# A block of gate and up in one pass, and the last LoRA unit woven with two down units

## What is computed

```python
h = layernorm(x) * (1 + ca) + sa
x = x + ga * scan_block(h)                 # selective scan, 16 states per feature
h = layernorm(x) * (1 + cb) + sb
gate = h @ gate_w.T + (h @ gate_a.T) @ gate_b.T
up   = h @ up_w.T   + (h @ up_a.T) @ up_b.T
hidden = silu(gate) * up                   # 2752 wide
x = x + gb * (hidden @ down_w.T + (hidden @ down_a.T) @ down_b.T)
```

## Time and profile before

| | |
|---|---|
| median of three runs | 2287.67 us |
| the profiled execution | 2279.5 us |
| its span | 2277.7 us |
| mean granted TensorE clock | 0.947 |
| busy: PE, PEld | 2044.7 us (90%), 1860.5 us (82%) |
| busy: DVE, ACT, POOL | 1442.4 (63%), 1041.2 (46%), 1542.8 (68%) |
| matmuls | 11652 |
| the chain that ended last, by engine | PE 55%, DVE 13%, POOL 9%, ACT 8%, issue 7%, DMA 6% |

### The profile page before, as it was taken

One profiled execution on the slowest core, in us unless ns is written; L12 is line 12 of the kernel. 1 busy time (PEld: TensorE's weight loads), 2 busy tenths in 40 slices (PEclk: granted clock), 3 DMA queues, 4 the chain that ended last, 5 costly groups with the idle time before them and its releaser, 6 DMA issues.

```text
span 2277.7 us, 33011 instructions
## 1 busy us (share of the span) xinstructions
PE 2044.7 (90%) x11652; PEld 1860.5 (82%) x11652; DVE 1442.4 (63%) x2119; ACT 1041.2 (46%) x2330; POOL 1542.8 (68%) x960
## 2 busy tenths in 40 slices
PE   7587756878879989899999899999899999999999
PEld 4233235778869989799999799999799999999999
DVE  4665776778767878767778667778667774211111
ACT  3776765666554555444545344555343332210000
POOL 1578779998988877877867777867869895110100
PEclk9688877989989999999999999999999999999999
DMA  9799875778967768586768586768587877787786
GB/s 361 301 359 342 309 289 211 279 266 277 340 248 277 255 241 283 207 274 219 246 225 280 178 280 224 242 224 284 171 268 257 280 258 256 253 287 275 253 291 218
DMA packets 121204, 602.99 MB, mean 265 GB/s; under 512 B 10576, under 2 KB 23120, under 8 KB 80464
## 3 DMA queue, kind: packets, MB, share of 16 engines
q1 hardware_dynamic: 121040, 600.89, 75.0%
HBM read 514.63 MB, written 86.21 MB: 264 GB/s over the span
## 4 chain that ended last, share of the span: by engine, by line
PE 55%; DVE 13%; POOL 9%; ACT 8%; issue 7%; DMA 6%; DVEq 0%; SPq 0%; ACTq 0%; POOLq 0%
PE FP L780 48%; DVE ring L1186 5%; POOL ring L1300 4%; PE FP L663 4%; POOL y L1275 2%; DVE ring L1071 2%; DMA raw<-w_gu 2%; ACT SC L851 2%; DVE FP L1161 2%; DMA wts<-w_scratch 2%; PE FP L804 1%; POOL wts L1283 1%; ACT sqb L969 1%; PE FP L741 1%; DMA w_scratch<-wts 1%
## 5 line engine op out<-in xcount | busy, mean ns | idle before, releaser
L780 PE MATMUL FP<-xhi,wts 128*128 128x368 f32 (+2 forms) x4320 | 1078.4, 326 | 62.9 <-ACT dtb L974 29.6
L780 PEld LDWEIGHTS FP<-xhi,wts 128*128 128x128 f32 x4320 | 774.1, 194 | 73.2 <-issue 61.5
L1300 POOL TENSOR_TENSOR ring<-ring,c_row 128x736 f32<-128x736 f32 (+2 forms) x336 | 575.7, 1714 | 236.0 <-ACT hst L868 235.7
L780 PE MATMUL FP<-xlo,wts 128*128 128x368 f32 (+2 forms) x2160 | 700.3, 324 | 0.0
L851 ACT ACTIVATE SC<-dtb,aneg 128x368 f32<-128x368 f32 (+2 forms) x768 | 409.4, 538 | 592.9 <-DVE ring L1186 592.6
L780 PE MATMUL FP<-hhi,wts 128*128 128x368 f32 (+5 forms) x2376 | 571.1, 321 | 27.6 <-POOL hlo L1315 23.2
L1186 DVE TENSOR_TENSOR_SCAN ring<-SC,hst,ring 128x368 f32<-128x368 f32 (+1 forms) x640 | 579.3, 946 | 3.6 <-ACT SC L851 3.6
L1275 POOL TENSOR_TENSOR y<-y,ring 128x736 f32<-128x736 f32 (+1 forms) x320 | 554.7, 1733 | 13.9
L780 PEld LDWEIGHTS FP<-hhi,wts 128*128 128x128 f32 (+1 forms) x2376 | 406.7, 185 | 34.9 <-POOL hlo L1315 22.3
L780 PEld LDWEIGHTS FP<-xlo,wts 128*128 128x128 f32 x2160 | 418.8, 194 | 1.1
L780 PE MATMUL FP<-hlo,wts 128*128 128x368 f32 (+5 forms) x1188 | 379.4, 319 | 0.0
(11 more groups left out here) (104 smaller groups left out, 1929.7 us busy)
## 6 DMA issues: line engine op xcount, KB each, us to landing
wts<-w_scratch SPq DMA_DIRECT2D x249, 1152.0 KB, 5.3
wts<-w_scratch SPq DMA_DIRECT2D x91, 896.0 KB, 5.0
wts<-w_scratch SPq DMA_DIRECT2D x51, 1024.0 KB, 5.5
w_scratch<-wts SPq DMA_DIRECT2D x44, 1152.0 KB, 8.6
raw<-w_gu SPq DMA_DIRECT2D x44, 576.0 KB, 6.8
modw<-mod_w SPq DMA_DIRECT2D x24, 1024.0 KB, 10.4
w_scratch<-wts SPq DMA_DIRECT2D x16, 896.0 KB, 6.8
w_scratch<-wts SPq DMA_DIRECT2D x9, 1024.0 KB, 7.8
```

Of the source, the lines that this page charges most:

```text
L780: last = mm(out, w, x, start=(start and k == 0 and e == 0), stop=(stop and k == n - 1 and e == 2))
L1300: G.tensor_tensor(buf, buf, over_pair(c_of(k)), ALU.mult).then_inc(g_hc, 1)
```

## The change

Three things change.

1. Gate and up of block 21 are one unit `both`: 64 columns of gate and 64 of up weights side by side, 25 matmuls instead of 50. There are 71 units. The up half comes out on partitions 64 to 127 of the bank; ScalarE copies it to `tda[0:64]` (new line 1041), and VectorE multiplies from there (new line 1241).
2. The third `lora_down` and the first two `down` units of that part are woven on TensorE: all but the last block of `lora_down`, all but the last block of down 0, the last block of `lora_down`, all but the last of down 1, then the last blocks of down 0 and down 1.
3. The pieces of those two `down` units move ahead of that `lora_down`, on all engines.

```diff
-        UNITS += [("gate", part, j), ("up", part, j)]
+        UNITS += [("gate", part, j), ("up", part, j)] if j < NH - 1 else [("both", part, j)]
...
+    for u in (LAST_LORA + 1, LAST_LORA + 2):
+        at[LAST_LORA] += at[u]
+        at[u] = []
     return at
...
-            g = item[1] * NU + item[2] + (2 if UNITS[item[2]][0] == "gate" else 1)
+            g = item[1] * NU + item[2] + (2 if UNITS[item[2]][0] == "gate" or item[2] == LAST_LORA else 1)
...
-                    unit(c, u)
+                    if u == LAST_LORA:
+                        for v, step in ((u, "begin"), (u + 1, "begin"), (u, "end"), (u + 2, "begin"), (u + 1, "end"), (u + 2, "end")):
+                            unit(c, v, step)
+                    elif u not in (LAST_LORA + 1, LAST_LORA + 2):
+                        unit(c, u)
...
+                elif kind == "both":
+                    act.wait_ge(pe_unit, g + 1)
+                    act.wait_ge(g_hlo, c * NH + j - 1)
+                    A(hid[0:HALF, j % 2, 0:T], FP[0:HALF, BANK["unit", c, u], 0:T], ACT.Tanh, scale=0.5).then_inc(a_th, 1)
+                    A(tda[0:HALF, 0:T], FP[HALF:P, BANK["unit", c, u], 0:T], ACT.Copy).then_inc(a_up, 1)
...
+                elif kind == "both":
+                    h = hid[0:HALF, j % 2, 0:T]
+                    dve.wait_ge(a_th, c * NH + j + 1)
+                    V.scalar_tensor_tensor(out=h, in0=h, scalar=1.0, in1=FP[0:HALF, BANK["unit", c, u], 0:T], op0=ALU.add, op1=ALU.mult).then_inc(v_half, 1)
+                    dve.wait_ge(v_half, c + 1)
+                    dve.wait_ge(a_up, c + 1)
+                    V.scalar_tensor_tensor(out=h, in0=h, scalar=0.5, in1=tda[0:HALF, 0:T], op0=ALU.mult, op1=ALU.mult).then_inc(v_used, 1)
...
+    w_gu[NH - 1, 0, :, :, HALF:] = w_gu[NH - 1, 1, :, :, 0:HALF]
```

More of the change, by code:

```diff
@@ L57 @@
     for j in range(k0 + (part > 0), min(k1 + 1, NH)):
-        UNITS += [("gate", part, j), ("up", part, j)]
+        UNITS += [("gate", part, j), ("up", part, j)] if j < NH - 1 else [("both", part, j)]
     UNITS += [("lora_down", part, 0)] + [("down", part, m) for m in range(ND)]
 NU = len(UNITS)
-LAST_UP = max(u for u, unit in enumerate(UNITS) if unit[0] == "up")
+BOTH = max(u for u, unit in enumerate(UNITS) if unit[0] == "both")
+HALF = HID % P
+assert 2 * HALF == P
 GU_COLS = (ND + 1) * P
@@ L81, in lo_cols @@
     n = PARTS[part][1] - PARTS[part][0]
-    return {"lora_a": ND * P, "gate": GU_COLS, "up": GU_COLS, "lora_down": n * TD_COLS, "down": n * P}[kind]
+    return {"lora_a": ND * P, "gate": GU_COLS, "up": GU_COLS, "both": GU_COLS, "lora_down": n * TD_COLS, "down": n * P}[kind]
 def raw_cols(u):
@@ L91, in passes @@
     n = PARTS[part][1] - PARTS[part][0]
-    return {"lora_a": 3 * ND, "gate": 3 * ND + 1, "up": 3 * ND + 1}.get(kind, 3 * n)
+    return {"lora_a": 3 * ND, "gate": 3 * ND + 1, "up": 3 * ND + 1, "both": 3 * ND + 1}.get(kind, 3 * n)
 LN_ORDER = [(0, 0), (0, 1), (1, 0)] + [x for c in range(1, CHUNKS) for x in ([(0, c + 1)] if c + 1 < CHUNKS else []) + [(1, c)]]
@@ L270 @@
 SCAN_SHARE = 0.985
+LAST_LORA = unit_at("lora_down", len(PARTS) - 1, 0)
 def pieces_at(c):
@@ L781, in products, with unit @@
                 return last
-            def unit(c, u):
+            def unit(c, u, step=None):
                 kind, part, j = UNITS[u]
@@ L788, in unit @@
                 k0, k1 = PARTS[part]
[L789 to L794, removed]
+                if step != "end":
+                    if g in OTF:
+                        pe.wait_ge(a_hi, OTF.index(g) + 1)
+                        pe.wait_ge(g_lo, OTF.index(g) + 1)
+                    else:
+                        pe.wait_ge(d_w[s], 16 * loads_until(g))
+                    bank_free(pe, "unit", c, u)
                 if kind == "lora_a":
                     pe.wait_ge(g_h2, PAIRS * (c + 1))
-                if kind in ("lora_a", "gate", "up"):
+                if kind in ("lora_a", "gate", "up", "both"):
                     out = FP[:, bank, 0:T]
@@ L811, in unit @@
                     out = FP[0:w, bank, 0:T]
-                    products(out, pairs[:-1], stop=False)
+                    if step != "end":
+                        if kind == "lora_down":
+                            pe.wait_ge(g_hlo, c * NH + k1 - 1)
+                        products(out, pairs[:-1], stop=False)
+                    if step == "begin":
+                        return
                     if kind == "lora_down":
                         pe.wait_ge(g_hlo, c * NH + k1)
-                    if part == len(PARTS) - 1 and kind == "down" and j == 0:
+                    if u == LAST_LORA + 1:
                         pe.wait_ge(v_hlo, c + 1)
@@ L872, in hi_part @@
                 last = A(hi[:, 0:w], src[:, 0:w], ACT.Copy)
-                if UNITS[u][0] in ("gate", "up"):
+                if UNITS[u][0] in ("gate", "up", "both"):
                     last = A(hi[64:128, w:], src[64:128, w:], ACT.Copy)
@@ L1043, in _ @@
                     last = UNITS[(g - 1) % NU][0] if g else None
-                    if last == "lora_a":
+                    if last in ("lora_a", "both"):
                         before(*divmod(g - 1, NU))
@@ L1053, in _ @@
                         split_hi(g + AHEAD_HI)
-                    if last == "up":
+                    if last in ("up", "both"):
                         after(*divmod(g - 1, NU))
@@ L1311, in after @@
                 T = CH[c]
-                if kind == "up":
+                if kind in ("up", "both"):
+                    rows = slice(0, P if kind == "up" else HALF)
                     pool.wait_ge(a_hh, c * (NH + 1) + j + 1)
                     k = j % PART_MAX
-                    G.tensor_tensor(hlo[:, k, 0:T], hid[:, j % 2, 0:T], hhi[:, k, 0:T].bitcast(F32), ALU.subtract).then_inc(g_hlo, 1)
+                    G.tensor_tensor(hlo[rows, k, 0:T], hid[rows, j % 2, 0:T], hhi[rows, k, 0:T].bitcast(F32), ALU.subtract).then_inc(g_hlo, 1)
             for p in FIRST:
```

12 lines of the change are left out of this document (7 added, 5 removed).

## The result

The changed kernel takes 2277.48 us (median of 5 runs, 2275.9 to 2280.25) against 2287.67 us (5 runs, 2286.38 to 2294.39): ratio 0.9963, interval 0.9949 to 0.9977. The profiled execution took 2278.67 us, its span is 2276.9 us, its clock 0.947.

The account below looks back on a forecast made before the run. Matmuls bound chunks 3 to 5, POOL chunk 0, with chunks 1 and 2 between. Gains of 8.4 + 12.0 + 1.5 + 2.6 = 24.5 us from the 2287.67 us median gave 2263 us, range 2251 to 2277.

Parts of the forecast that it names:

- The matmuls taken out: Each chunk loses 25 matmuls, one gate or up unit; 23.35 us if all of it lies on the path.
- The end of chunks 1 to 3: Old stall goes, two new ones (3.9 and 1.7 us) come; only the unit's price is gained, 12.0 us in all.
- The stretch before chunk 0: One of 48 weight preparations falls away before chunk 0: 2.6 us gained, between nothing and some 5 us.
- Moved for nothing: Bank and piece numbers shift by one unit; bank waits of 29.6 us may move a few us either way: 0.
- The end of chunk 0: POOL bounds chunk 0; half a unit gained, 1.5 us, between 2 us worse (late weights) and 4.5 us better.
- The boundary gives back its unit: Rival: new stalls at chunk ends longer than worked out; chunks 0 to 3 give nothing, 2276.7 us; chance 0.15.
- The stalls go: Rival: squares ready sooner or POOL ahead; chunks 0 to 3 give 3 us more each, 2251 us; chance 0.12.
- The chunk start takes it back: Rival: the chain ending in the `xlo` wait is the bound; chunks 0 to 4 give nothing, 2281 us; chance 0.04.
- Slower: Rival: POOL two groups behind at the ends of chunks 0 to 3, `hlo` 7.1 us later, 2297 us; chance 0.04.
- The port lock: Rival: second multiply of `both` waits for a POOL instruction in chunks 0 to 3; 7.1 us, 2270; chance 0.07.
- its own sign of the lock: Profile sign: second multiply of `both` over 1 us long, or late with POOL busy, would show the forecast wrong.
- 4.5 us beside the sum: Two gaps per boundary, each bringing back the half clock, would make the sum 3 x 1.5 = 4.5 us smaller.

Follow-up runs that it names:

- the old places: Changed kernel, but the planner counts the merged unit as 50 matmuls, so scan pieces stand at the units where they stood before: 2267.57 us (0.9924).
- the new ones: Scan pieces where the changed kernel's planner puts them (2277.48 us, 0.9963); the kernel before with only these places: 2297.89 us (1.0050).
- the last table: Profiles by chunk, x load two units later: kernel before 2277.03 us; with pieces at their former units, merged unit alone 2262.45, whole change 2252.57.
- the best version: Changed kernel with pieces at the units where they stood before and the x load of chunk c + 2 two units later: 2252.57 us (0.9864).
- putting back one bunch: Changed kernel with only the pieces of units 16 to 20 put back where they stood before: 2279.07 us (0.9974).
- the later load: The x load of chunk c + 2 asked for two units later: on the kernel before 2277.03 us (0.9969), on the changed kernel 2269.07 (0.9936).

## Why the prediction was wrong

**Right.** The matmuls taken out, 150. Chunk 5: 4.1 us for a forecast of 4.18; chunk 4: 4.6 at the old places, 3.0 at the new ones. "The end of chunks 1 to 3": two stalls, at the squares and at `hlo`, in the places forecast, 3.22 and 0.37 us for 3.9 and 1.7, and 22.9 us for 23.6 in all. As a sum over chunks it holds, roughly, only for chunks 2 and 3, and only in the last table (3.2 us each for 4.18): chunk 1 gives 0.5 there for 3.66, chunk 0 nothing for 1.5. The stretch before chunk 0 was mis-sized the other way: 2.6 forecast, with 5 as the upper end. Six profiles with the old units start chunk 0 at 363.4 to 368.8 us, eleven with the merged unit at 356.8 to 362.3, means 365.9 and 358.9: 7 us. So where the best version gains its 24 us, chunks 0 to 3 give 6.4 us for a forecast of 13.5, and the start makes up for it: that it comes to the forecast's 24.5 us is luck.

**Wrong: "Moved for nothing".** This is the step that failed. That paragraph gave 0 us to the pieces' shift by a unit, with "either way by a few us" for the bank waits. It is 9 us in the changed kernel (0.9963 against 0.9924) and 11 us in the kernel before (1.0050). It came not in the row I looked at, the bank waits of 29.6 us, which fell to 25.5, but as waits for `hb`, `hid` and `xs` that the profile of before hardly had. Which pieces cost what stays open: putting back one bunch gave nothing.

**Wrong: the cover of the weights.** In "The end of chunk 0" I sized late weights at 2 us, by the end of `lora_down` and the load's 5.6 us of the earlier trace rows. The stall is elsewhere, 18 us behind the cut that begins chunk 1, behind an x load that stands for the landing of the last outputs. With the later load, in both kernels, the change at the old places gains 24 us, without it 17. So 7 us are lost there, and with the 9 us of the places that comes to the gap between 24.5 and the 8.5 us of the ratio. The split hangs on the order: with the load moved first it is worth nothing to the change, and the places then cost 0.9936 - 0.9864, 17 us.

**The rivals.** "The boundary gives back its unit" came nearest by its number, 2276.7, but not by its mechanism: the boundary's waits are near the forecast's or below, and that of chunk 3 gave 5.2 us. "The stalls go" is half true: `hlo` all but went, the squares did not. "The chunk start takes it back" named the start of a chunk but `xlo`, whose waits did not change (19.0 to 19.8). "Slower" has no trace: `hlo` waits 5.1 us in all.

**The port lock.** The second multiply of `both` took 482/635/1283 ns (minimum, median, maximum), the first one, from PSUM, 412/528/529:

```profile
L1241 DVE SCALAR_TENSOR_TENSOR hid<-hid,tda x6: 482/635/1283, 633.6 to 2239.1; 64x368 f32<-64x368 f32 x4, 64x256 f32<-64x256 f32 x1, 64x320 f32<-64x320 f32 x1
L1238 DVE SCALAR_TENSOR_TENSOR hid<-hid,FP x6: 412/528/529, 633.1 to 2238.5; 64x368 f32<-64x368 f32 x4, 64x256 f32<-64x256 f32 x1, 64x320 f32<-64x320 f32 x1
```

The rows at the end of chunk 3 show what holds it up:

```profile
1640.73 0.96 POOL L1348 TENSOR_TENSOR hlo<-hid,hhi 128x368 fp32r<-128x368 f32 x1
1640.80 1.28 DVE L1241 SCALAR_TENSOR_TENSOR hid<-hid,tda 64x368 f32<-64x368 f32 x1
1641.64 2.05 POOL L1307 TENSOR_TENSOR y<-y,ring 128x736 f32<-128x736 f32 x1
1642.01 1.74 DVE L1154 SCALAR_TENSOR_TENSOR hb<-FP,y 128x736 f32<-128x736 f32 x2
```

POOL's subtraction had begun 0.07 us earlier, and the multiply took 0.75 us more than its 0.53 in chunks 4 and 5, where POOL was idle. It is the same in chunk 2. In chunk 1 the multiply began first and took 0.48 us, and POOL's subtraction beside it 1.14 where its neighbour took 0.88. The Trainium skill, page "SBUF — State Buffer", section "SBUF: two separate sides", says that whichever of the two, a VectorE instruction with two SBUF inputs or a GpSimd one that reads SBUF, starts first keeps the ports that they share for its whole instruction, and the other is blocked; so the later one waits for what is left of it. These rows agree. The prediction priced a POOL multiply of 1.78 us in each of four chunks; met was what was left of a subtraction of 0.96. But its own sign of the lock, a second multiply over 1 us long, is there in chunks 2 and 3. Nor is the cost hidden: the centring (L1154) starts when the multiply ends, the squares follow it, and TensorE waits 3.22 us for them. By the rows some 0.75 us of that wait is the lock's, an estimate that no run tests.

**The clock.** The gap of 3.22 us was followed by a clock of 0.61 and cost 4.43 - 2.63 = 1.8 us more; the one of 0.37 us by none. The Trainium skill, page "TensorE: Matmul & The Clock Gate", section "HAM oscillation", by which I had put 4.5 us beside the sum, holds here for one gap of the two; the section speaks of long gaps, which the prediction had left out.

## What to carry to other kernels

When a change alters a number that a planner divides by, all work that the planner places moves: compare the orders everywhere, not only at the edit, and time the old kernel with the new places alone, or the new one with the old; each is a line. On a queue that issues in order, ask of every wait what stands behind it: while the x load waited for a landing, from 685.8 to 693.2 us here, no load of weights was issued. And profile the old kernel twice: a stall that comes in one execution and not in another is missing from a sum built on one.

## What had not been expected

The same wait can cost different things. At the end of chunk 2 TensorE stood 2.34 us for `xlo` in both kernels; before, `lora_a` then ran at full clock, in the changed kernel not (the stretches begin 0.1 us ahead of the first matmul behind the wait):

```profile
1343.50:1347.80 4.30, 4.24 (x25) 4.27 (x26) 3.37 (x4) 2.43 (x6) 4.22 (x3) 1.00 0.90 325
```

```profile
1347.50:1353.40 5.90, 5.84 (x25) 5.87 (x26) 3.37 (x4) 2.42 (x6) 5.82 (x4) 0.71 0.72 233
```

The first is of the kernel before, the second of the changed one, which took 1.6 us longer for the same 25 matmuls. Gains of two edits did not add either: the later x load is worth 7 us to the kernel before, 6 with the weave, 4 with the merged unit at the old places, and 14 with both there.
